# A transformer block on one core: the 128-column score row as one full-precision product, placed last, with a reordered ScalarE and VectorE

## The chip, the cores and the metric

One NeuronCore of one Trainium2 chip runs the whole kernel. The time is the device time of one execution in microseconds. Engine names: PE is TensorE, ACT is ScalarE, DVE is VectorE, POOL is GpSimd.

## What is computed

The reference, cut to what matters here (B = 16 batches of S = 512 tokens, width 128, 16 heads of 64, 8 experts with hidden size 512):

```
h = layernorm(x) * (1 + ca) + sa
q, k, v = h @ W_Q, h @ W_K, h @ W_V                  # 16 heads of 64 columns
scores  = q @ k.T / 8, causal mask, softmax over keys  # 512 x 512 for each head
x = x + ga * ((probs @ v) @ W_out + b_out)
h = layernorm(x) * (1 + cb) + sb
w = softmax over the 2 largest of h @ Wr + br
x = x + gb * sum_e w_e * (gelu(h @ W1_e + b1_e) @ W2_e + b2_e)
```

Everything is float32 in and out.

## The kernel before

**Stages.** The attention of all 16 batches comes first, then the experts of all 16 batches. In attention a batch is worked through in 8 pairs of heads, numbered 0 to 7 here; so there are 128 pairs, each the same pipeline. The change lies in this stage alone.

**Products in parts.** Most products are made of three reduced-precision products of a high and a low part: hi*hi, hi*lo, lo*hi. For q and k, ACT rounds the product in PSUM to the high part (`round_q`, `round_k`), and DVE subtracts it to get the low part (`rest_q`, `rest_k`, semaphores `q_lo` and `k_lo`). The buffers `q_hi2`, `q_lo2`, `k_hi2`, `k_lo2` hold two pairs.

**Rows and units.** The causal scores of a head are four query blocks of 128 rows. Row r needs (r + 1) * 128 key columns. They are made in three units (`UNITS`): row 3 (512 columns); rows 2 and 0 (384 and 128); row 1 (256). Each unit has its own two PSUM banks, one for each head of the pair. The two heads lie in different halves of the partitions, so their products use different halves of the array's rows (line 578).

**What PE does in a pair p**, in this order: scores of pair p in three units; `weigh_values` of pair p-2 (line 605, probabilities times V, full precision); `project_q` and `project_k` of pair p+1 (lines 523 to 525); up to two chunks of V (the same lines), none in pairs 2 and 6, two in pairs 0 and 3, one in the others; in pair 2 and pair 6 the output projection (lines 627 to 629); then 40 transposes of the probabilities of pair p-1 (line 592), in groups 2, 0, 1. The group 2 waits for all eight normalised rows of pair p-1 (`p_norm`).

**What the others do around it.** DVE (`front`, `rear`) inverts the softmax sums of pair p-1 (line 1246), adds the mask and takes the row maximum of all eight rows of pair p (line 1237), makes the low parts of z, q and k, and copies two of the three groups of transposes out of PSUM (line 1230). ACT takes the exponentials with their sums (line 954), rounds z, q and k (lines 966, 935, 939), copies the V chunks out of PSUM (line 979), and copies the third group of transposes (line 945). POOL waits for the inverted sums (`rden`) and multiplies the eight rows by them (line 501, `p_norm`). PE reads `v_done` of the last V chunk of a pair before the scores of the next, since that chunk and the score row 3 use one bank. A unit of scores waits by `t_dve` until DVE has copied the transposes that lay in its banks: unit 1 for the first copy, unit 2 for the second.

Each engine follows its own written order, and semaphores alone join them; there is no planner.

Of the kernel before, what the change touches and what calls it, by code (L numbers as in the profile page):

```python
# [17 lines left out]


ROW_ORDER = [3, 2, 0, 1]  # L20
UNITS = [[3], [2, 0], [1]]
ROW_AT = {3: 0, 2: 512, 0: 896, 1: 1024}
ROW_IN_BANK = {3: 0, 2: 0, 0: 384, 1: 0}
HEAD_COLS = 1280


# [17 lines left out]

def masked_at(h, u):

    return (h, 2 + 2 * h, 6 + h)[u]


AHEAD = [[], [2, 3], [2, 3], [2, 3], [2, 3], [2], [], [2]]  # L50
# [7 lines left out]
def adaln_moe_kernel(nc, resid, W_Q, W_K, W_V, W_out, b_out, W1, b1, W2, b2, Wr, br, c_in, wmod, out):  # L58
# [10 lines left out]
    with ExitStack() as ctx:  # L69
# [3 lines left out]
        def sem(name):  # L73
            return ctx.enter_context(nc.semaphore(name))
# [98 lines left out]
        with ExitStack() as pa:  # L173
            def sa(name, shape, dt=F32):
                return sb(name, shape, dt, pa)
# [23 lines left out]
        with ExitStack() as pb:  # L199
# [29 lines left out]
            neg_max = sa("neg_max", [P, 2, 8])  # L229
            denom = sa("denom", [P, 2, 8])  # L230
            rdenom = sa("rdenom", [P, 2, 8])

            raw_w = [v_sb[:, i, :] for i in range(3)]
            raw_wo = hidden[:, 1, 2:4, :].rearrange("p c s -> p (c s)")
# [119 lines left out]
            z_rounded = sem("z_rounded")  # L354

            q_lo = sem("q_lo")
            k_lo = sem("k_lo")
            t_dve = sem("t_dve")
            s_masked = sem("s_masked")
# [13 lines left out]
            with nc.Block() as block:  # L373
# [66 lines left out]
                @block.gpsimd  # L440
                def _(pool):
                    def inv_std(b):

                        wait_alone(pool, ln_mv, NT * b + NT)
                        pool.tensor_scalar(var_eps[:, :], meanvar[:, :, 1], EPS, 1.0, ALU.add, ALU.mult)\
                            .then_inc(ln_eps, 1)
                        pool.wait_ge(ln_eps, b + 1)
                        pool.tensor_tensor(rstd[:, :], var_eps[:, :], neg_half[:, :], ALU.pow).then_inc(ln_rstd, 1)

                    pool.memset(ident[:, :], 0.0).then_inc(pool_zero, 1)  # L450
                    pool.memset(mask_w[:, :], 0.0).then_inc(pool_zero, 1)
                    pool.memset(neg_half[:, :], -0.5).then_inc(pool_const, 1)
                    pool.wait_ge(pool_zero, 2)
                    pool.affine_select(out=ident[:, :], in_=ident[:, :], compare_op=ALU.not_equal, fill=1.0,
                                       base=0, pattern=[[-1, P]], channel_multiplier=1).then_inc(pool_const, 1)

                    pool.affine_select(out=mask_w[:, 384:512], in_=mask_w[:, 384:512], compare_op=ALU.is_ge,
                                       fill=NEG, base=0, pattern=[[-1, P]], channel_multiplier=1)\
                        .then_inc(pool_const, 1)
                    pool.wait_ge(pool_const, 1)  # L460
                    inv_std(0)
                    wo_v = W_out.rearrange("c (n two) d -> two c n d", two=2)
                    for half in range(2):
                        pool.dma_start(raw_wo[half * DH:(half + 1) * DH, :].rearrange("p (n d) -> p n d", n=NP),
                                       wo_v[half]).then_inc(load_w[3], 16)
                    pool.dma_start(bo_col[:, :], b_out.rearrange("(d o) -> d o", o=1)).then_inc(load_kept, 16)
                    pool.dma_start(br_b[:, :], br.partition_broadcast(P)).then_inc(load_kept, 16)
                    pool.dma_start(wr_sb[:, :], Wr).then_inc(load_kept, 16)
                    pool.wait_ge(load_kept, 48)

                    def router_inv_std(b):

                        wait_alone(pool, r_mv, NT * b + NT)
                        pool.tensor_scalar(var_eps[:, :], meanvar[:, :, 1], EPS, 1.0, ALU.add, ALU.mult).then_inc(r_eps, 1)
                        pool.wait_ge(r_eps, b + 1)
                        pool.tensor_tensor(rstd[:, :], var_eps[:, :], neg_half[:, :], ALU.pow).then_inc(r_rstd, 1)

                    def summed(b, e):

                        return (E - 1) * b + e  # L480

                    def add_expert(b, e):
                        wait_alone(pool, y_weighted, expert(b, e) + 1)
                        if e > 1:

                            wait_alone(pool, y_summed, summed(b, e - 1))
                        pool.tensor_tensor(acc[:, :], acc[:, :], y_w[:, :], ALU.add).then_inc(y_summed, 1)  # L487

                    def body(b, first, last):
                        for p in range(NP):  # L490
                            if p == 2 and not last:
                                inv_std(b + 1)
                            if p == 2 and last:
                                router_inv_std(0)

                            wait_alone(pool, rden, pair(1, b, p) + 1)
                            for h in range(2):
                                for r in ROW_ORDER:
                                    at, n = ROW_AT[r], (r + 1) * P
                                    part = probs[:, p % 2, h, at:at + n]  # L500
                                    pool.tensor_scalar(part, part, rdenom[:, p % 2, 4 * h + r:4 * h + r + 1], 1.0,  # L501
                                                       ALU.mult, ALU.mult)\
                                        .then_inc(p_norm, 1)

                    batches(pool, body)

                    def experts(b, first, last):
                        if not first:
                            add_expert(b - 1, E - 1)
                        if not last:  # L510
                            router_inv_std(b + 1)
                        if first:
                            pool.wait_ge(oT_ps, B)
                        for e in range(1, E - 2 if last else E - 1):
                            add_expert(b, e)

                    batches(pool, experts)

                @block.tensor
                def _(pe):  # L520
# [38 lines left out]
                    def scores(b, p, u, begin, young):  # L559
# [3 lines left out]
                            pe.wait_ge(k_lo, pair(1, b, p) + 1)  # L563
                        if young and not begin:

                            pe.wait_ge(s_masked, (2, 6, 8)[u])
                        if not young and u > 0:

                            pe.wait_ge(t_dve, pair(2, b, p) - (3, 2)[u - 1])
                        for r in UNITS[u]:  # L570
                            n = (r + 1) * P
                            at = ROW_IN_BANK[r]
                            rows = slice(r * P, (r + 1) * P)
# [35 lines left out]
                    def values(b, p, n, i):  # L609

                        t, half = i % 4, (i // 4) % 2
                        if i == 8:
                            pe.wait_ge(h_rest, b + 2)

                        pe.wait_ge(s_masked, pair(8, b, p) + (7, 2)[n])
                        toks, cols = slice(t * P, (t + 1) * P), slice(half * 512, half * 512 + 512)
                        split_product(V_BANK[n], (h_hi[:, toks], h_lo[:, toks]),
                                      (wv[0][:, cols], wv[1][:, cols])).then_inc(v_ps, 1)
# [97 lines left out]
                    def body(b, first, last):  # L716
                        for p in range(NP):
# [52 lines left out]
                                router_logits(0, k_bank)  # L770
                                project_out(b, 0, done + 2, range(2))
                            if not begin:
                                pe.wait_ge(s_masked, done + 6)
                                if p == 4 and last:
                                    attention_T_beside(b - 1)
                                if p == 5 and last:
# [143 lines left out]
                def _(act):  # L920
# [155 lines left out]
                    def front(b, p, first, last):  # L1076
# [7 lines left out]
                            round_q(*nxt, False)  # L1084
                            round_k(*nxt)
                        exponentials(b, p, 0, 1)
                        exponentials(b, p, 1, 1, [2])
                        if not (first and p < 2):
                            round_z(*two_before(b, p))
                        if has_next and not begin:  # L1090
# [7 lines left out]
                            round_w(1, 0)  # L1098
                            round_w(1, 1)
                        put = chunk_banks(p, first, last)  # L1100
                        if now:
                            values_out(b, put[0], now[0])
                        exponentials(b, p, 1, 1, [0])
                        exponentials(b, p, 0, 2)

                    def rear(b, p, first, last):
# [1 line left out]
                        prev = before(b, p)  # L1108
                        now = chunks(p, first, last)
                        put = chunk_banks(p, first, last)  # L1110
                        for n, i in zip(put[1:], now[1:]):
                            values_out(b, n, i)
                        exponentials(b, p, 1, 2)
                        if p == 5 and last:
                            act.wait_ge(t_dve, pair(2, *prev) + 1)
                            router_h_evac(0, in_halves(hf[:, :]), side)
# [3 lines left out]
                            router_round_h(0)  # L1120
                        if not begin:
                            evac_T(*prev, first and p == 1)
                        if begin:
                            round_weights(3)

# [64 lines left out]
                def _(dve):  # L1190
# [249 lines left out]

                    def front(b, p, first, last):
                        begin, nxt = first and p == 0, after(b, p)
                        if not begin:
                            invert_sums(*before(b, p))
                        mask_and_max(b, p, 0, 0)
                        mask_and_max(b, p, 1, 0)
                        mask_and_max(b, p, 0, 1)
                        if begin:
                            rest_q(*nxt)
# [141 lines left out]
```

## Time and profile before

| what | value |
|---|---|
| median of 3 runs | 1885.24 us (1884.66 to 1886.86) |
| the profiled execution's own time | 1885.15 us |
| its span | 1883.4 us, granted TensorE clock 0.997 |
| PE busy | 1869.1 us, 99% of the span |
| DVE, ACT, POOL busy | 1649.5, 1559.0, 731.9 us |
| attention stage, first scores to last transposes | 14.88 to 1148.6 us |

Busy time of PE is a union of instructions that overlap: a matmul of 512 columns is shown as 0.39 us long, while the next one starts 0.23 us after it. So a late start of up to about 0.16 us leaves no gap in PE's busy time. Distances between starts are read here instead.

### The profile page before, as it was taken

How to read it: one execution, taken by the hardware profiler on the slowest of the kernel's cores; microseconds unless marked ns; L12 is line 12 of the kernel's file. 1: busy time of each engine (PE TensorE's matmuls, PEld its weight loads, DVE VectorE, ACT ScalarE, POOL GpSimd, SP SyncE). 2: the span in 40 equal slices, each digit the busy share in tenths (PEclk: the TensorE clock that was granted, in tenths of full speed). 3: DMA queues.
4: the chain of work that ended last, by engine and by line, in shares of the span. 5: the costliest groups of instructions: out<-in, count | busy, mean ns of one | idle time of the engine just before them, and what ended most of it. 6: DMA issues, size and time to landing. Idle time of an engine off the chain costs nothing.

```text
span 1883.4 us, 50582 instructions
## 1 busy us (share of the span) xinstructions
PE 1869.1 (99%) x15334; PEld 1431.1 (76%) x15334; DVE 1649.5 (88%) x4388; ACT 1559.0 (83%) x3664; POOL 731.9 (39%) x1212
## 2 busy tenths in 40 slices
PE   8999999999999999999999999999999999999999
PEld 6777777777777777777777777888888888888887
DVE  7888888888888888888888888998998899899998
ACT  7888988988988988988988988777777777777775
POOL 4454454454444444544544442222222222222221
PEclk9999999999999999999999999999999999999999
DMA  4100000000000000000000003111111111111111
GB/s 129 62 2 1 1 1 0 1 1 0 1 1 0 1 1 0 1 1 0 1 1 1 1 2 91 52 51 50 50 50 50 50 50 50 50 50 50 51 55 52
DMA packets 42622, 50.04 MB, mean 27 GB/s; under 512 B 3160, under 2 KB 24464, under 8 KB 42512
## 3 DMA queue, kind: packets, MB, share of 16 engines
q1 hardware_dynamic: 42256, 48.41, 8.1%
q0 software_dynamic: 256, 0.53, 0.1%
q14 instruction: 86, 0.70, 0.1%
q8 instruction: 24, 0.39, 0.1%
HBM read 44.47 MB, written 4.46 MB: 26 GB/s over the span
## 4 chain that ended last, share of the span: by engine, by line
PE 97%; DVE 1%; issue 1%; ACT 1%; POOL 0%; DMA 0%; ACTq 0%; SPq 0%; DVEq 0%
PE banks L605 16%; PE banks L578 13%; PE banks L592 9%; PE banks L684 6%; PE banks L686 6%; PE banks L685 6%; PE banks L703 6%; PE banks L705 6%; PE banks L704 6%; PE banks L523 6%; PE banks L525 5%; PE banks L524 5%; PE banks L627 2%; PE banks L628 2%; PE banks L629 2%
## 5 line engine op out<-in xcount | busy, mean ns | idle before, releaser
L501 POOL TENSOR_SCALAR probs<-probs,rdenom 128x512 f32<-128x512 f32 (+3 forms) x1024 | 525.9, 540 | 586.3 <-DVE rdenom L1246 586.3
L954 ACT ACTIVATE probs<-probs,neg_max 128x512 f32<-128x512 f32 (+3 forms) x1024 | 561.6, 551 | 56.4 <-DVE neg_max L1237 56.4
L1059 ACT ACTIVATE hidden<-banks,b_cols 128x512 f32<-128x512 f32 x512 | 350.3, 689 | 177.2 <-PE banks L686 176.9
L1237 DVE CUSTOM_DVE_ANT_0 probs<-banks,mask_w 128x512 f32<-128x512 f32 (+3 forms) x1024 | 427.1, 482 | 3.9 <-PE banks L578 0.6
L1416 DVE TENSOR_TENSOR hid_lo<-hidden,hid_hi 128x512 fp32r<-128x512 f32 x512 | 380.5, 754 | 56.7 <-ACT hid_hi L1067 41.9
L487 POOL TENSOR_TENSOR acc<-acc,y_w 128x512 f32<-128x512 f32 x110 | 151.5, 1378 | 462.6 <-DVE y_w L1429 460.9
L605 PE MATMUL banks<-probs_T,v_sb 128*64 128x512 f32 (+3 forms) x2048 | 305.6, 441 | 0.3 <-issue 0.3
L1230 DVE COPY probs_T<-banks 128x512 f32<-128x512 f32 (+1 forms) x256 | 232.6, 949 | 29.7 <-PE banks L592 29.7
L605 PEld LDWEIGHTS banks<-probs_T,v_sb 128*64 128x64 f32 x2048 | 136.7, 137 | 156.3 <-issue 120.0
L592 PEld LDWEIGHTS banks<-ident,probs 64*128 64x128 f32 x5120 | 171.7, 140 | 45.5 <-issue 45.4
L684 PE MATMUL banks<-h_hi,w_hi 128*128 128x512 f32 x512 | 205.7, 402 | 0.1
L685 PE MATMUL banks<-h_hi,w_lo 128*128 128x512 f32 x512 | 199.6, 390 | 0.0
L686 PE MATMUL banks<-h_lo,w_hi 128*128 128x512 f32 x512 | 199.6, 390 | 0.0
L703 PE MATMUL banks<-hid_hi,w_hi 128*128 128x512 f32 x508 | 197.8, 389 | 0.0
L705 PE MATMUL banks<-hid_lo,w_hi 128*128 128x512 f32 x508 | 197.7, 389 | 0.0
L704 PE MATMUL banks<-hid_hi,w_lo 128*128 128x512 f32 x508 | 197.6, 389 | 0.0
L954 ACT ACTIVATION_READ_ACCUMULATOR probs<-probs,neg_max 128x1 f32 x1024 | 192.5, 188 | 0.0
L592 PE MATMUL banks<-ident,probs 64*128 64x64 f32 x5120 | 189.2, 226 | 0.8 <-ACT hidden L1059 0.6
L578 PE MATMUL banks<-k_hi,q_hi 64*128 64x512 f32 (+3 forms) x1024 | 177.3, 342 | 4.2 <-DVE probs_T L1230 2.1
L1250 DVE TENSOR_TENSOR z_lo<-banks,z_hi 128x512 fp32r<-128x512 f32 x128 | 88.3, 690 | 90.3 <-ACT z_hi L966 88.4
L578 PE MATMUL banks<-k_hi,q_lo 64*128 64x512 f32 (+3 forms) x1024 | 166.0, 319 | 0.0
L945 ACT ACTIVATE probs_T<-banks 128x1024 f32<-128x1024 f32 x128 | 129.8, 1014 | 43.5 <-PE banks L592 43.5
(182 smaller groups left out, 3425.9 us busy)
## 6 DMA issues: line engine op xcount, KB each, us to landing
w_rows<-w_kept SPq DMA_DIRECT2D x128, 256.0 KB, 4.3
x_all<-in_L_attn_resid_dram SPq DMA_DIRECT2D x16, 256.0 KB, 2.7
w_raw<-in_L_ffn_W_dram SPq DMA_DIRECT2D x16, 256.0 KB, 4.7
out_dram<-y_result SPq DMA_DIRECT2D x15, 256.0 KB, 2.3
v_sb<-in_L_attn_W_V_dram SPq DMA_DIRECT2D x1, 512.0 KB, 5.7
hidden<-in_L_attn_W_out_dram POOLq DMA_DIRECT2D x2, 256.0 KB, 6.4
v_sb<-in_L_attn_W_Q_dram SPq DMA_DIRECT2D x1, 448.0 KB, 3.4
v_sb<-in_L_attn_W_K_dram SPq DMA_DIRECT2D x1, 448.0 KB, 4.4
```

The costliest lines, as they stand in the source:

```text
L501: pool.tensor_scalar(part, part, rdenom[:, p % 2, 4 * h + r:4 * h + r + 1], 1.0, ALU.mult, ALU.mult)\
L578: mm = pe.matmul(S_BANK[u][h][:, at:at + n], q[own, p % 2, rows], k[own, p % 2, 0:n], start=start, stop=stop)
L592: mm = pe.transpose(banks[:, first_bank + half, at:at + DH], probs[own, p % 2, h, src:src + P], ident[own, own])
L605: mm = pe.matmul(bank[h * DH:(h + 1) * DH, c * P:S], v_sb[:, c, hc:hc + DH], probs_T[:, h, KEY_AT[c]:KEY_AT[c] + n], start=(c == 0), stop= ...
L684: pe.matmul(banks[:, c, :], w1_hi[:, e, cols], h_hi[:, :], start=True, stop=False)
L685: pe.matmul(banks[:, c, :], w1_lo[:, e, cols], h_hi[:, :], start=False, stop=False)
L686: pe.matmul(banks[:, c, :], w1_hi[:, e, cols], h_lo[:, :], start=False, stop=True)\
L703: pe.matmul(y_bank, w2_hi[:, e, c, :], hi, start=(c == 0), stop=False)
L954: act.activation(part, part, ACT.Exp, bias=neg_max[:, p % 2, col:col + 1], scale=-1.0, accum_out=denom[:, p % 2, col:col + 1]).then_inc(p_ ...
L1059: act.activation(hidden[:, e % 2, c, :], banks[:, c, :], ACT.Gelu, bias=b1_cols[:, e * HC + c:e * HC + c + 1]).then_inc(hid, 1)
L1237: dve.tensor_tensor_reduce(out=probs[:, p % 2, h, at:at + n], in0=S_BANK[u][h][:, col:col + n], in1=mask_w[:, 512 - n:512], scale=-SCALE, ...
L1416: dve.tensor_tensor(hid_lo[:, e % 2, c, :], full, hi.bitcast(F32), ALU.subtract)\
```

## The change

Score row 0 moves out of the middle unit to the end of the last one, behind row 1, and becomes one full-precision float32 product of `q_full` and `k_full` per head instead of three products of parts. POOL makes `q_full` and `k_full` (128 columns each) as the sum of the high and the low part, behind its eight multiplications of a pair, and tells by `q_whole` and `k_whole`. ACT copies both V chunks of a pair ahead of the last exponentials, and copies its group of transposes ahead of the last head's exponentials (two of them now). DVE inverts the sums of the pair before behind the first two masks instead of ahead of them. Semaphore counts follow.

```diff
-UNITS = [[3], [2, 0], [1]]
+UNITS = [[3], [2], [1, 0]]
-ROW_IN_BANK = {3: 0, 2: 0, 0: 384, 1: 0}
+ROW_IN_BANK = {3: 0, 2: 0, 0: 256, 1: 0}
...
-    return (h, 2 + 2 * h, 6 + h)[u]
+    return (h, 2 + h, 4 + 2 * h)[u]
...
                                         .then_inc(p_norm, 1)
+                            if not (last and p >= NP - 2):
+                                join(*after(*after(b, p)))
+
+                    def join(b, p):
+
+                        wait_alone(pool, q_lo, pair(1, b, p) + 1)
+                        pool.tensor_tensor(q_full[:, p % 2, :], q_hi2[:, p % 2, 0:P].bitcast(F32),
+                                           q_lo2[:, p % 2, 0:P].bitcast(F32), ALU.add).then_inc(q_whole, 1)
+                        wait_alone(pool, k_lo, pair(1, b, p) + 1)
+                        pool.tensor_tensor(k_full[:, p % 2, :], k_hi2[:, p % 2, 0:P].bitcast(F32),
+                                           k_lo2[:, p % 2, 0:P].bitcast(F32), ALU.add).then_inc(k_whole, 1)
+
+                    join(0, 0)
+                    join(0, 1)
                     batches(pool, body)
...
-                            pe.wait_ge(s_masked, (2, 6, 8)[u])
+                            pe.wait_ge(s_masked, (2, 4, 8)[u])
...
                         for r in UNITS[u]:
+                            if r == 0:
+                                pe.wait_ge(q_whole, pair(1, b, p) + 1)
+                                pe.wait_ge(k_whole, pair(1, b, p) + 1)
+                                at = ROW_IN_BANK[0]
+                                for h in range(2):
+                                    own = slice(h * DH, (h + 1) * DH)
+                                    mm = pe.matmul(S_BANK[u][h][:, at:at + P], q_full[own, p % 2, :],
+                                                   k_full[own, p % 2, :], start=True, stop=True)
+                                continue
...
-                        pe.wait_ge(s_masked, pair(8, b, p) + (7, 2)[n])
+                        pe.wait_ge(s_masked, pair(8, b, p) + (6, 2)[n])
...
-                                pe.wait_ge(s_masked, done + 6)
+                                pe.wait_ge(s_masked, done + 4)
...
                         exponentials(b, p, 0, 1)
-                        exponentials(b, p, 1, 1, [2])
+                        exponentials(b, p, 1, 1)
...
-                        if now:
-                            values_out(b, put[0], now[0])
-                        exponentials(b, p, 1, 1, [0])
+                        for bank, i in zip(put[:2], now[:2]):
+                            values_out(b, bank, i)
                         exponentials(b, p, 0, 2)
...
-                        for n, i in zip(put[1:], now[1:]):
+                        for n, i in zip(put[2:], now[2:]):
                             values_out(b, n, i)
-                        exponentials(b, p, 1, 2)
+                        if begin:
+                            exponentials(b, p, 1, 2)
...
                         if not begin:
                             evac_T(*prev, first and p == 1)
+                            exponentials(b, p, 1, 2)
...
                         begin, nxt = first and p == 0, after(b, p)
+                        mask_and_max(b, p, 0, 0)
+                        mask_and_max(b, p, 1, 0)
                         if not begin:
                             invert_sums(*before(b, p))
-                        mask_and_max(b, p, 0, 0)
-                        mask_and_max(b, p, 1, 0)
                         mask_and_max(b, p, 0, 1)
```

## Rows read from the trace of the kernel before

**Rows 1.** The profile's page: span, chain that ended last, two groups of POOL.

```profile
span 1883.4 us, 50582 instructions
PE 97%; DVE 1%; issue 1%; ACT 1%; POOL 0%; DMA 0%; ACTq 0%; SPq 0%; DVEq 0%
L487 POOL TENSOR_TENSOR acc<-acc,y_w 128x512 f32<-128x512 f32 x110 | 151.5, 1378 | 462.6 <-DVE y_w L1429 460.9
```

**Rows 2.** Waits of PE: who waited for whom; us in total, times, longest.

```profile
PE banks L592 <- POOL probs L501: 0.2, 1, 0.2
```

**Rows 3.** Timeline of PE, scores of one pair 3; start us, length us, what.

```profile
602.79 0.48 PE L578 MATMUL banks<-k_hi,q_hi 64*128 64x512 f32 x2
...
603.92 0.33 PE L578 MATMUL banks<-k_lo,q_hi 64*128 64x384 f32 x2
604.10 0.22 PE L578 MATMUL banks<-k_hi,q_hi 64*128 64x128 f32 x2
...
604.38 0.34 PE L578 MATMUL banks<-k_hi,q_hi 64*128 64x256 f32 x2
604.55 0.28 PE L578 MATMUL banks<-k_hi,q_lo 64*128 64x256 f32 x2
604.67 0.28 PE L578 MATMUL banks<-k_lo,q_hi 64*128 64x256 f32 x2
604.88 2.38 PE L605 MATMUL banks<-probs_T,v_sb 128*64 128x512 f32 x16
```

**Rows 4.** Timeline of PE: a run of full-precision products of 128 columns.

```profile
12.90 2.05 PE L798 MATMUL banks<-mask_w,ident 128*128 128x128 f32 x16
```

**Rows 5.** Timeline of DVE, pairs 3 to 5.

```profile
602.40 1.81 DVE L1230 COPY probs_T<-banks 128x512 f32<-128x512 f32 x2
...
612.37 0.19 DVE L1246 RECIPROCAL rdenom<-denom 128x8 f32<-128x8 f32 x1
612.67 0.69 DVE L1237 CUSTOM_DVE_ANT_0 probs<-banks,mask_w 128x512 f32<-128x512 f32 x1
...
613.90 0.55 DVE L1237 CUSTOM_DVE_ANT_0 probs<-banks,mask_w 128x384 f32<-128x384 f32 x1
...
618.30 0.69 DVE L1223 TENSOR_TENSOR k_lo<-banks,k_hi 128x512 fp32r<-128x512 f32 x1
```

**Rows 6.** Timeline of POOL: eight multiplications each, in pairs 4 and 5.

```profile
612.73 4.10 POOL L501 TENSOR_SCALAR probs<-probs,rdenom 128x512 f32<-128x512 f32 x8 [4.14 <-DVE rdenom L1246]
621.00 4.10 POOL L501 TENSOR_SCALAR probs<-probs,rdenom 128x512 f32<-128x512 f32 x8 [4.18 <-DVE rdenom L1246]
```

**Rows 7.** Timeline of PE: transposes and the scores behind them, pairs 3 to 5.

```profile
610.13 1.49 PE L592 MATMUL banks<-ident,probs 64*128 64x64 f32 x40
611.56 0.50 PE L578 MATMUL banks<-k_hi,q_hi 64*128 64x512 f32 x2
...
618.25 1.48 PE L592 MATMUL banks<-ident,probs 64*128 64x64 f32 x40
619.53 0.48 PE L578 MATMUL banks<-k_hi,q_hi 64*128 64x512 f32 x2
...
626.20 1.47 PE L592 MATMUL banks<-ident,probs 64*128 64x64 f32 x40
```

**Rows 8.** Timeline of ACT, end of pair 3 and end of pair 6.

```profile
610.93 0.58 ACT L979 ACTIVATE v_sb<-banks 128x512 f32<-128x512 f32 x1
611.40 0.50 ACT L954 ACTIVATE probs<-probs,neg_max 128x256 f32<-128x256 f32 x1
...
638.58 1.03 ACT L945 ACTIVATE probs_T<-banks 128x1024 f32<-128x1024 f32 x1 [0.51 <-PE banks L592]
```

**Rows 9.** Timelines at the end of attention: ACT, POOL, PE.

```profile
1140.02 1.02 ACT L945 ACTIVATE probs_T<-banks 128x1024 f32<-128x1024 f32 x1 [0.87 <-PE banks L592]
...
1141.11 5.07 POOL L501 TENSOR_SCALAR probs<-probs,rdenom 128x512 f32<-128x512 f32 x8 [5.32 <-DVE rdenom L1246]
...
1146.33 0.47 PE L592 MATMUL banks<-ident,probs 64*128 64x64 f32 x8 [0.20 <-POOL probs L501]
```

More of the change, by code:

```diff
@@ L231, in adaln_moe_kernel @@
             rdenom = sa("rdenom", [P, 2, 8])
+            q_full = sa("q_full", [P, 2, P])
+            k_full = sa("k_full", [P, 2, P])
             raw_w = [v_sb[:, i, :] for i in range(3)]
@@ L356, in adaln_moe_kernel @@
             q_lo = sem("q_lo")
+            q_whole, k_whole = sem("q_whole"), sem("k_whole")
             k_lo = sem("k_lo")
```

## The prediction, made before the changed kernel ran

> **What bounds the kernel now.** First the page: the chain that ended last is PE for 97% of the span [rows 1]. Then the waits of PE: POOL made it wait once, for 0.2 us, in the whole run [rows 2]. Both say that PE alone sets the time, and both hide how near the others are. So I read, third, the timelines of each engine over one batch and lay them side by side, all measured from the first score matmul of a pair (call it S). The first scores stand at 14.88 us and the experts begin at about 1149, so a pair takes some 8.8 us on average, and by the timeline a pair with one V chunk (pairs 1, 4, 5, 7) takes 7.97: pair 4 runs from 611.56 to 619.53 [rows 7].
>
> In pair 4 the transposes start at 618.25, S + 6.69 [rows 7]. They need all eight rows of the pair before from POOL. POOL works from 612.73 for 4.10 us, to 616.83 [rows 6]: 1.42 us early. In pair 5 they start at 626.20, S + 6.67, and POOL ends at 625.10: 1.10 us early. This slack is the number on which everything below turns. POOL starts 0.17 us behind the end of the reciprocal (612.37 + 0.19 = 612.56, then 612.73) [rows 5, 6].
>
> **Row 0 on PE.** Before, in its place: row 2's last product starts at 603.92, row 0's first at 604.10 and row 1's first at 604.38, so row 0 costs 0.28 us for three products of both heads, side by side [rows 3]. Row 1's three start at 604.38, 604.55, 604.67: 0.17 and 0.12 apart, where the first is longer since its weights were only being loaded behind row 0's short products. From row 2's last start to row 1's last start it is 0.75 us. After: row 1's weights load beneath row 2's 384 columns, so 0.17 to its first product and 0.12 twice; then row 0. A full-precision product shows as two instructions. A run of 16 of 128 columns lasts 2.05 us; with 0.38 off for the last one's length and the first weight load, 15 steps in 1.67, 0.11 each [rows 4]. The products of probabilities and V are full precision too, two heads in different columns of the array: 16 instructions in 2.38 us [rows 3] is 8 steps, the heads side by side. If the heads are side by side here as well, row 0 is 0.12 + 0.11, and the sum from row 2's last start to the last start of the unit is 0.17 + 0.24 + 0.12 + 0.11 = 0.64, 0.11 less than 0.75. The trace has no full-precision product of two heads in different rows of the array. The bounds: side by side, -0.11 us for a pair; one head behind the other, four steps instead of two, +0.11. I take the first, since line 578's own products and line 605's both run in step.
>
> The row speaks of weight loads (0.11 a step) as the limit at 128 columns. The Trainium skill, FP8 and Floating Point Precision, section TensorE Precision Notes, says that true FP32 takes four passes through the array (H*H + H*L + L*H + L*L). By that count the product would grow from three passes to four of 128 columns, and would lose where I have it gain; a step of 0.11 for two passes of 128 columns fits its count, but the three reduced products took 0.28, not the 0.16 of three passes, so here the count does not set the price.
>
> The two new waits ahead of row 0: what is queued behind is row 0, then `weigh_values`. `k_lo` of pair 5 ends at 618.30 + 0.69 = 618.99 [rows 5]; POOL wakes 0.17 later and adds. Its addition of 128 columns is bounded from above by one of 512 columns, 1.38 us [rows 1], from below by nothing. So `k_whole` comes at 619.2 to 620.5, and row 0 is due at S + 1.5 = 621.0 [rows 7]. No cost at either end. POOL's additions stand behind its multiplications, and POOL then idles 4.1 us [rows 6]: no cost either.
>
> **The second V chunk.** In pair 3 ACT ends it at 610.93 + 0.58 = 611.51, and the scores start at 611.56 [rows 7, 8]: 0.05 us is the way from ACT to PE. Transposes to scores is 1.43 us there (610.13 to 611.56) against 1.28 in pair 4 (618.25 to 619.53), and the late scores pay 0.02 more for weights not loaded ahead. One exponential of about 0.4 us stands ahead of the chunk that then stands behind. So 0.17 us goes in pairs 0 and 3 each. Next in line there is PE itself.
>
> **Transposed copy ahead of exponentials, on ACT.** Where ACT is free it starts this copy at S + 0.23 (638.58 in pair 7, with its scores at 638.35) and takes 1.03 [rows 8]. The two exponentials moved behind it (0.49 and 0.39 to their next) end at about S + 2.15, plus 0.05 on the way. Now the sums of the pair before are complete only there, instead of before S.
>
> **The reciprocal moved on DVE.** This is the step that costs. Before, it ran ahead of the masks: 612.37 in pair 4, S + 0.81, and at S + 1.11 in pair 5 (POOL's 621.00 less 0.17 and 0.19 [rows 6]). After, it stands behind two masks of 512 columns, which start at S + 1.09 to 1.11, when unit 0 is done (612.67 in pair 4), and take to 613.90, 1.23 us [rows 5]. So: 1.09 + 1.23 = S + 2.32 (the exponentials' S + 2.20 is hidden by it), + 0.19 for itself, + 0.17 until POOL starts = 2.68, + 4.10 = 6.78, + 0.15 from POOL's end to the transposes (1141.11 + 5.07 = 1146.18, then 1146.33 [rows 9]) = S + 6.93. PE would be there at 6.67 - 0.11 = 6.56. So pairs 1, 4, 5, 7 start their transposes at 6.93, not at 6.67 or 6.69: 0.25 us later than before, whatever PE gains in row 0. What is queued behind the wait is all that remains of the pair and the next pair's scores: a closed loop of scores, masks, reciprocal, POOL, transposes, 6.93 + 1.28 = 8.21 us instead of 7.96. In pairs 0, 2, 3, 6 PE has a second V chunk or a projection to do first, arrives at 7.2 or later (pair 3: 610.13 - 602.79 = 7.34, less 0.11) and is not held.
>
> **The unit moved forward.** Row 1 now starts behind row 2 and needs the second DVE copy out of its banks. In pair 3 it ends at 602.40 + 1.81 = 604.21, + 0.05 = S + 1.47 [rows 5]; with 0.11 for the weights the first product of row 1 can start at S + 1.58, and before it started at 1.59 (604.38), just free. Now it is due at 603.92 + 0.17, S + 1.30 [rows 3]: 0.28 us lost. This is in pair 3 only. Elsewhere the copy ends 2.3 us behind the transposes' start (610.13, and 612.37 + 0.08 for the reciprocal behind it [rows 5, 7]), which is S + 1.04 of the next pair, where the transposes themselves are what DVE waits for.
>
> **The sum for a batch**: pairs 1, 4, 5, 7: 4 * 0.25 = +1.0. Pairs 2 and 6: -0.22. Pair 0: -0.11 - 0.17 = -0.28. Pair 3: -0.11 - 0.17 + 0.28 = 0. Together +0.5; times 16, +8.0. The first batch has DVE further behind and its loop is later for it: +1, my estimate. At the end of attention ACT waits 0.87 us for its transposes (to 1140.02) with the exponentials done [rows 9]; now two of them come behind, so the sums, POOL and ACT's next work are some 0.9 later, and PE waits there already: +0.9. Sum +9.9, on the profiled execution's own 1885.15 (span 1883.4, 1.75 around it), which lies 0.1 below the median: 1895.1 us.
>
> **Rivals.** (1) *The heads of row 0 run one behind the other.* For: nothing in the trace shows them side by side in this form. Against: rows 3. It costs 0.22 more where PE is the bound, pairs 0, 2, 3, 6: 64 * 0.22 = 14; in the others 6.78 stays below 6.93. 1909. Four passes by count, 0.05 more instead of 0.11 less, would give 64 * 0.16 = 10 more, 1905. (2) *The loop through POOL doesn't bind, and the change brings what PE gains.* It needs POOL's end at S + 6.4 instead of 6.78, as when the reciprocal starts by S + 1.95: between the masks, or with masks a third shorter. Against: three durations that hardly vary (masks, 4.10, 0.15). From 0.38 us less it decides, and the time is the other side's: -0.11 in eight pairs, -0.17 in two, +0.28 in pair 3, and some 0.08 back in four for the copy that unit 2 now waits for: -0.6 a batch, -10, 1875. (3) *The loop binds, but less*, as latencies overlap: half the 0.25 gives 64 * 0.12 = 8 less, 1887, hardly told from no change.
>
> **How the numbers follow.** Forecast, with its own range 1890 to 1900: 0.62. Rival 1 with its form by passes: 0.16. Rival 2: 0.10. Rival 3: 0.12. A measurement of this kernel tells 0.2%, 3.8 us. Faster by more: rival 2, 0.10. Within: most of rival 3, 0.10. Slower: 0.80. The range, 1887 to 1906, leaves out rival 2 and the serial end of rival 1.
>
> **What would show it.** Right: waits of PE on POOL's line 501, about 64 of them, in pairs 1, 4, 5, 7; transposes at S + 6.9 there; reciprocal at S + 2.3; POOL's end 0.15 ahead of the transposes. Line 578's last unit 0.64 long from row 2's last start; row 0's two heads within 0.01 us. Pair 3 to 4: transposes to scores 1.28, and a DVE wait at unit 2 in pair 3. Wrong: no wait on POOL, or masks that start ahead of S + 1.0.

## The result, and the profile after

| | before | changed |
|---|---|---|
| median (19 runs each) | 1885.11 us (1882.86 to 1887.39) | 1889.87 us (1887.97 to 1891.26) |
| ratio to the kernel before, 95% interval | | 1.0025 (1.0018 to 1.0031) |
| span of the profiled execution | 1883.4 us | 1889.4 us |

Slower by 4.8 us, where 1895.1, slower by 9.9, was forecast. The direction and the mechanism came out, the size did not.

The page of the changed kernel (span; busy times; the chain; one group of POOL):

```profile
span 1889.4 us, 50738 instructions
...
PE 1856.6 (98%) x15078; PEld 1424.6 (75%) x15078; DVE 1669.1 (88%) x4388; ACT 1563.9 (83%) x3664; POOL 850.2 (45%) x1468
...
PE 96%; issue 2%; DVE 1%; ACT 1%; POOL 0%; DMA 0%; ACTq 0%; DVEq 0%; POOLq 0%
```

PE is busy for 12.5 us less and the kernel takes longer: the gain on PE is there, and "issue" has grown from 1% to 2% [rows 1]. The waits of PE in the changed kernel (us in total, times, longest) say where:

```profile
PE banks L617 <- issue: 19.0, 64, 1.1
...
PE banks L603 <- DVE probs_T L1256: 1.6, 5, 0.3
PE banks L617 <- POOL probs L504: 1.4, 1, 1.4
```

Line 617 are the transposes (592 before). They waited 64 times: 56 times in pairs 1, 4, 5, 7 of the 14 middle batches, about 0.27 us each, and eight times in the first and the last batch, the longest 1.06 us; before, once [rows 2]. The view puts this down to "issue": a bare wait instruction stands between POOL's signal and the transposes, and only the timelines of both engines show who ended it. First PE, pair 3 to pair 5, which answers to [rows 3, 7]:

```profile
607.84 0.34 PE L603 MATMUL banks<-k_lo,q_hi 64*128 64x384 f32 x2
608.18 0.39 PE L603 MATMUL banks<-k_hi,q_hi 64*128 64x256 f32 x2
...
614.20 1.47 PE L617 MATMUL banks<-ident,probs 64*128 64x64 f32 x40
615.48 0.48 PE L603 MATMUL banks<-k_hi,q_hi 64*128 64x512 f32 x2
...
616.62 0.33 PE L603 MATMUL banks<-k_lo,q_hi 64*128 64x384 f32 x2
616.79 0.28 PE L603 MATMUL banks<-k_hi,q_hi 64*128 64x256 f32 x2
616.91 0.28 PE L603 MATMUL banks<-k_hi,q_lo 64*128 64x256 f32 x2
617.02 0.28 PE L603 MATMUL banks<-k_lo,q_hi 64*128 64x256 f32 x2
617.14 0.38 PE L593 MATMUL banks<-k_full,q_full 64*128 64x128 f32 x4
617.46 2.37 PE L630 MATMUL banks<-probs_T,v_sb 128*64 128x512 f32 x16
...
622.38 1.43 PE L617 MATMUL banks<-ident,probs 64*128 64x64 f32 x39 [0.28 <-issue]
623.61 0.47 PE L603 MATMUL banks<-k_hi,q_hi 64*128 64x512 f32 x1
...
630.54 1.48 PE L617 MATMUL banks<-ident,probs 64*128 64x64 f32 x40 [0.27 <-issue]
```

Then DVE and POOL in the same stretch, which answers to [rows 5, 6]:

```profile
606.31 1.81 DVE L1256 COPY probs_T<-banks 128x512 f32<-128x512 f32 x2
...
616.58 0.69 DVE L1263 CUSTOM_DVE_ANT_0 probs<-banks,mask_w 128x512 f32<-128x512 f32 x1
...
617.81 0.20 DVE L1272 RECIPROCAL rdenom<-denom 128x8 f32<-128x8 f32 x1
```

```profile
618.18 4.10 POOL L504 TENSOR_SCALAR probs<-probs,rdenom 128x512 f32<-128x512 f32 x8 [3.31 <-DVE rdenom L1272]
622.33 0.46 POOL L513 TENSOR_TENSOR q_full<-q_hi,q_lo 128x128 f32<-128x128 f32 x1
622.92 0.46 POOL L516 TENSOR_TENSOR k_full<-k_hi,k_lo 128x128 f32<-128x128 f32 x1
626.34 4.10 POOL L504 TENSOR_SCALAR probs<-probs,rdenom 128x512 f32<-128x512 f32 x8 [2.96 <-DVE rdenom L1272]
```

In pair 4 the scores start at 615.48 (S), the masks at S + 1.10, the reciprocal at S + 2.33, POOL runs from S + 2.70 to 622.28 = S + 6.80, and the transposes start at S + 6.90: 0.10 behind POOL. This is the closed loop. Row 0 at 617.14 has both heads side by side: four instructions in 0.38 us.

The distance from scores to scores, pair by pair, read from the starts on PE's timeline (medians of batches 2 to 14; us):

```
pair          0     1     2     3     4     5     6     7
before      8.78  7.97  9.99  8.78  7.97  7.95 10.87  7.95
forecast    8.50  8.22  9.88  8.78  8.22  8.20 10.76  8.20
changed     8.54  8.16  9.91  8.78  8.13  8.18 10.79  8.14
```

A batch takes 70.64 us instead of 70.27, +0.37, where +0.5 was forecast. Of the 5 us by which the forecast was too high, 1.8 lie in these middle batches and the rest in the first batch and at the end of attention, worked out below.

### The profile page after: what moved, and what is told of

It reads as the page before. It is cut to its first block, busy times and chain, and to the rows that moved or that the text cites. A ratio compares the mean times of both kernels' runs of the same rounds, so it can differ in the third digit from the quotient of the medians.

```text
span 1889.4 us, 50738 instructions
## 1 busy us (share of the span) xinstructions
PE 1856.6 (98%) x15078; PEld 1424.6 (75%) x15078; DVE 1669.1 (88%) x4388; ACT 1563.9 (83%) x3664; POOL 850.2 (45%) x1468
## 4 chain that ended last, share of the span: by engine, by line
PE 96%; issue 2%; DVE 1%; ACT 1%; POOL 0%; DMA 0%; ACTq 0%; DVEq 0%; POOLq 0%
PE banks L630 15%; PE banks L603 11%; PE banks L617 9%; PE banks L709 6%; PE banks L710 6%; PE banks L711 6%; PE banks L728 6%; PE banks L730 6%; PE banks L729 6%; PE banks L539 6%; PE banks L540 5%; PE banks L541 4%; PE banks L652 2%; PE banks L653 2%; PE banks L654 2%
## 5 line engine op out<-in xcount | busy, mean ns | idle before, releaser
L1263 DVE CUSTOM_DVE_ANT_0 probs<-banks,mask_w 128x512 f32<-128x512 f32 (+3 forms) x1024 | 434.6, 480 | 6.9 <-PE banks L603 0.7
L1092 ACT ACTIVATE hid_hi<-hidden 128x512 fp32r<-128x512 f32 x256 | 161.0, 629 | 0.0
L603 PE MATMUL banks<-k_hi,q_hi 64*128 64x512 f32 (+2 forms) x768 | 150.4, 367 | 3.5 <-DVE q_lo L1243 1.6
```

The lines of the kernel that those rows point to most:

```text
L603: mm = pe.matmul(S_BANK[u][h][:, at:at + n], q[own, p % 2, rows], k[own, p % 2, 0:n], start=start, stop=stop)
L1263: dve.tensor_tensor_reduce(out=probs[:, p % 2, h, at:at + n], in0=S_BANK[u][h][:, col:col + n], in1=mask_w[:, 512 - n:512], scale=-SCALE, ...
```

## The experiments

The parts of the change were run alone and undone one by one, then the loop itself was lengthened, shortened and opened. Each ran in turn with the kernel before (1884 to 1885 us); ratios have 95% intervals. The changed kernel did not run again in these rounds: differences to it are taken from its median above, 1889.87, and since the kernel before was up to 1.25 us faster here than there, they are certain to about 1 us only. The theory under test: the added time comes only from the loop of scores, masks, reciprocal, POOL and transposes in the pairs 1, 4, 5, 7.

**The sooner V chunk alone.**

```diff
-                        if now:
-                            values_out(b, put[0], now[0])
+                        for bank, i in zip(put[:2], now[:2]):
+                            values_out(b, bank, i)
...
-                        for n, i in zip(put[1:], now[1:]):
+                        for n, i in zip(put[2:], now[2:]):
```

> The kernel before with one part alone: ACT copies both V chunks ahead of the last exponentials. The loop theory (the added time comes only from the loop scores, masks, reciprocal, POOL, transposes) has this part as a pure gain: transposes to scores 1.28 us instead of 1.43 in pairs 0 and 3, 0.17 us each with the weights, 32 times, -5.4 us. Rival, that ACT's order is where the changed kernel loses: then this is no gain or a loss, 0 or above.

1878.28 us, ratio 0.9964 (0.9950 to 0.9977), -6.7. Pairs 0 and 3 fall from 8.78 to 8.64, pairs 1 and 4 from 7.97 to 7.95. This part is a gain and by itself the faster kernel.

**The late reciprocal alone.**

```diff
-                        if not begin:
-                            invert_sums(*before(b, p))
                         mask_and_max(b, p, 0, 0)
                         mask_and_max(b, p, 1, 0)
+                        if not begin:
+                            invert_sums(*before(b, p))
```

> The kernel before with one part alone: the sums are inverted behind the first two masks. Loop theory: in pairs 1, 4, 5, 7 the transposes start at 6.9 us behind the scores' start instead of 6.67, about 0.2 us more each, 64 times, +13 us, and a few more in the first batch. Rival, that the loss comes from row 0's product or from ACT: then there is no change here, within 2 us.

1896.63 us, ratio 1.0060 (1.0047 to 1.0074), +11.6. Its timelines of POOL and PE at a pair 5:

```profile
629.91 4.10 POOL L501 TENSOR_SCALAR probs<-probs,rdenom 128x512 f32<-128x512 f32 x8 [4.07 <-DVE rdenom L1246]
```

```profile
634.11 1.47 PE L592 MATMUL banks<-ident,probs 64*128 64x64 f32 x40 [0.16 <-issue]
635.36 0.50 PE L578 MATMUL banks<-k_hi,q_hi 64*128 64x512 f32 x2
```

POOL ends at 634.01, the transposes start 0.10 later, 6.9 behind their scores. One reciprocal, moved behind two masks on DVE, costs more than the whole change does.

**Both of these.**

```diff
-                        if now:
-                            values_out(b, put[0], now[0])
+                        for bank, i in zip(put[:2], now[:2]):
+                            values_out(b, bank, i)
...
+                        mask_and_max(b, p, 0, 0)
+                        mask_and_max(b, p, 1, 0)
                         if not begin:
                             invert_sums(*before(b, p))
-                        mask_and_max(b, p, 0, 0)
-                        mask_and_max(b, p, 1, 0)
```

> The kernel before with two parts: the reciprocal behind the first two masks and the sooner V chunk. If the parts add up: +11.6 (the reciprocal alone) - 6.7 (V alone) = +4.9, 1889 to 1890, the changed kernel's own time, which means that row 0's place, its product and ACT's other order come to nothing together. If the late reciprocal takes away what the V chunk gives (the same pairs held by POOL): 1893 or more.

1891.01 us, ratio 1.0035 (1.0022 to 1.0049), +7.2 where the sum of the two is +4.9, which the interval just holds. So the two add up nearly or wholly, and what remains of the change (row 0's place, its product, ACT's other order) is worth about -1 us in all (1889.87 less 1891.01), or -2.4 if each kernel is held against the kernel before of its own round.

**Row 0 in parts, everything else as changed.**

```diff
-                            if r == 0:
-                                pe.wait_ge(q_whole, pair(1, b, p) + 1)
-                                pe.wait_ge(k_whole, pair(1, b, p) + 1)
...
-                                join(*after(*after(b, p)))
...
```

> The changed kernel, but row 0 stays three products of parts in its new place (last), and POOL makes no sums. Loop theory: pairs 1, 4, 5, 7 don't notice, since POOL holds them; pairs 0, 2, 3, 6 lose the 0.08 to 0.11 us that the one product gains: 64 * 0.1, +5 to +6 us against the changed kernel, 1895. Rival, that POOL's sums or the two added waits delay something: at or below the changed kernel.

1894.08 us, ratio 1.0050 (1.0037 to 1.0064): 4.2 above the changed kernel, where 5 to 6 was expected. Pairs 1, 4, 5, 7 are unchanged at 8.15 to 8.17, pairs 0, 2, 3, 6 are 8.61, 9.98, 8.87, 10.86, 0.07 to 0.09 more each. The one product gains where PE is the bound and nothing where POOL is. The rest of the remainder, place and ACT's order, costs about 3.

**Row 0 and the V chunk, with ACT and DVE in their old order.**

```diff
-                        if begin:
-                            exponentials(b, p, 1, 2)
+                        exponentials(b, p, 1, 2)
...
-                            exponentials(b, p, 1, 2)
...
+                        if not begin:
+                            invert_sums(*before(b, p))
                         mask_and_max(b, p, 0, 0)
...
```

> The changed kernel with two parts undone: the reciprocal ahead of the masks again, and ACT's last two exponentials ahead of its transposed copy again. Row 0's product and the sooner V chunk stay. Loop theory: POOL ends at 5.6 us behind the scores' start and holds nobody; the scores gain 0.08 in all eight pairs, 0.15 in pairs 0 and 3, and give 0.28 back in pair 3 where unit 2 waits for a DVE copy: -0.6 us a batch, about -10 against the kernel before, unless ACT's copy now comes too late for the weighted values. Rival, that row 0's product costs more than it saves: above the kernel before.

1889.68 us, ratio 1.0026 (1.0015 to 1.0036): a miss; I had named the doubt and put the time on the other side of it. With row 0 in the last unit, the last head has two exponentials ahead of ACT's transposed copy. PE in a pair 4 (its scores start at 615.10), then ACT:

```profile
615.10 0.47 PE L603 MATMUL banks<-k_hi,q_hi 64*128 64x512 f32 x1
...
617.27 2.38 PE L630 MATMUL banks<-probs_T,v_sb 128*64 128x512 f32 x16
```

```profile
616.17 1.00 ACT L970 ACTIVATE probs_T<-banks 128x1024 f32<-128x1024 f32 x1
```

The copy ends at 617.17, S + 2.07, and the weighted values start 0.10 later, at S + 2.17 instead of 1.98. The sums are complete late too, so the masks start at S + 1.41 instead of 1.10. The loop through POOL is open here (its end is at S + 5.73 in this pair and near 5.65 in most), and the time is the changed kernel's all the same.

**Row 0's part alone on the kernel before.**

```diff
-UNITS = [[3], [2, 0], [1]]
+UNITS = [[3], [2], [1, 0]]
...
+                                    mm = pe.matmul(S_BANK[u][h][:, at:at + P], q_full[own, p % 2, :],
...
```

> The kernel before with row 0's part alone (its place, the one product, POOL's sums), ACT and DVE in their old order. By the run that also had the sooner V chunk (1889.7): ACT has two exponentials of the last head ahead of its transposed copy, ends this at 2.08 us behind the scores' start, and the weighted values wait for it. Without the sooner V chunk pairs 0 and 3 pay more, since one exponential more stands ahead of it: 0.3 us or more each, +10 us against that run, 1899. Rival, that the product by itself is a gain: below 1885.

1890.61 us, ratio 1.0036 (1.0022 to 1.0050), 0.9 above the run before it and not 10. Pairs 0 and 3 pay 0.15 each for the late V chunk, half of what was expected; in return pairs 1 and 4 behind them take 7.85 and 7.87 instead of 8.03, since ACT has done one exponential more by then and its copy starts at S + 0.72 instead of 1.08. I had counted the first, at twice its size, and not the second. The rival falls too: row 0's part as a whole (place, product, sums) is no gain while ACT and DVE keep their old order. Of the product alone this run says nothing; the run with row 0 in parts does.

**The reciprocal put back, ACT as changed.**

```diff
+                        if not begin:
+                            invert_sums(*before(b, p))
                         mask_and_max(b, p, 0, 0)
                         mask_and_max(b, p, 1, 0)
-                        if not begin:
-                            invert_sums(*before(b, p))
```

> The changed kernel with the reciprocal alone put back ahead of the masks; ACT still takes the last head's two exponentials behind its transposed copy, so the sums are complete only at about 2.2 us behind the scores' start. DVE stands at the reciprocal until then: reciprocal from 2.2, POOL from 2.55 to 6.65, 0.15 earlier than in the changed kernel, but the masks begin at 2.4 instead of 1.1, and the exponentials, the rounding of z and what follows them on ACT come 1 us later. Loop theory with this: slower than the changed kernel, 1900 or more, so the move of the reciprocal is the price of ACT's order. Rival, that the place of the reciprocal alone is at fault: faster than the changed kernel.

1926.29 us, ratio 1.0223 (1.0209 to 1.0237). DVE's timeline in a pair 2:

```profile
614.96 0.20 DVE L1272 RECIPROCAL rdenom<-denom 128x8 f32<-128x8 f32 x1 [0.48 <-ACT probs L979]
615.16 0.69 DVE L1263 CUSTOM_DVE_ANT_0 probs<-banks,mask_w 128x512 f32<-128x512 f32 x1
```

DVE stands still for ACT's sums with eight masks queued behind. With ACT's order as changed, the reciprocal can't stay in front: the one move enforces the other. The loop through POOL does not explain this time, for POOL's end lies at S + 6.72 in a pair 4, ahead of the 6.80 of the changed kernel. There DVE, then PE:

```profile
634.47 0.20 DVE L1272 RECIPROCAL rdenom<-denom 128x8 f32<-128x8 f32 x1 [1.21 <-ACT probs L979]
...
639.84 0.68 DVE L1249 TENSOR_TENSOR k_lo<-banks,k_hi 128x512 fp32r<-128x512 f32 x1
```

```profile
640.67 0.50 PE L603 MATMUL banks<-k_hi,q_hi 64*128 64x512 f32 x2
```

DVE waits 1.21 us, then works without a gap from the reciprocal to the low part of k, which ends at 640.52, and the next scores, which need it, start 0.15 later. This is a second closed loop (scores, ACT's sums, reciprocal, masks, DVE's low parts), and it takes 8.39 us. Pairs 0, 2, 3 and 6 are 0.3 to 0.4 longer too; what holds them was not followed.

**One of POOL's eight multiplications left out.** Row 2 of the second head stays unnormalised.

```diff
                                 for r in ROW_ORDER:
+                                    if (h, r) == (1, 2):
+                                        continue
...
-                                wait_alone(pe, p_norm, pair(8, *prev) + 8)
+                                wait_alone(pe, p_norm, pair(7, *prev) + 7)
```

> The changed kernel, but POOL leaves out one of its eight multiplications (row 2 of the second head is not normalised), which takes 0.56 us off its 4.10. Loop theory: POOL ends at 6.25 instead of 6.8, PE reaches the transposes at 6.59 by itself, and pairs 1, 4, 5, 7 fall to 7.87 us: 0.3 us each, 64 times, -19 us against the changed kernel, so -14 against the kernel before. Rival, that POOL's work is off the path: no change against the changed kernel, +5 against the kernel before.

1871.73 us, ratio 0.9928 (0.9915 to 0.9942): -18.1 against the changed kernel, -19 expected. Its POOL and PE in a pair 4:

```profile
607.33 3.54 POOL L506 TENSOR_SCALAR probs<-probs,rdenom 128x512 f32<-128x512 f32 x7 [3.31 <-DVE rdenom L1274]
```

```profile
604.63 0.48 PE L605 MATMUL banks<-k_hi,q_hi 64*128 64x512 f32 x2
611.18 1.47 PE L619 MATMUL banks<-ident,probs 64*128 64x64 f32 x40
612.46 0.48 PE L605 MATMUL banks<-k_hi,q_hi 64*128 64x512 f32 x2
```

POOL ends at 610.87, PE reaches its transposes at S + 6.55 by itself: 7.83 us for the pair.

**One multiplication more.**

```diff
+            spare_cols = sa("spare_cols", [P, P])
...
                             wait_alone(pool, rden, pair(1, b, p) + 1)
+                            pool.tensor_scalar(spare_cols[:, :], ident[:, :], 1.0, 1.0, ALU.mult, ALU.mult)
```

> The changed kernel with one more multiplication of 128 columns on POOL, to a tile that nobody reads, ahead of its eight (some 0.36 us). Loop theory: pairs 1, 4, 5, 7 pay it in full, 64 * 0.36 = +23 us against the changed kernel, pairs 0 and 3 next to nothing, pairs 2 and 6 nothing: 1913. Rival, that POOL only happens to end there: no change, 1890.

1906.33 us, ratio 1.0116 (1.0100 to 1.0131): 16.5 above the changed kernel instead of 23. The added instruction and the next, on POOL:

```profile
634.71 0.30 POOL L501 TENSOR_SCALAR spare_cols<-ident 128x128 f32<-128x128 f32 x1 [2.96 <-DVE rdenom L1274]
634.98 4.08 POOL L506 TENSOR_SCALAR probs<-probs,rdenom 128x512 f32<-128x512 f32 x8
```

It takes 0.27 us and not 0.36. POOL's end moves by 0.25, from S + 6.79 to 7.04, pairs 1, 4, 5, 7 by 0.24 to 0.25 (8.38 to 8.42), the other four by 0.02 or less: 64 * 0.25 = 16. Only the instruction was priced too high.

**The sums inverted head by head.**

```diff
+                    def invert_head(b, p, h):
+                        dve.wait_ge(p_exp, pair(8, b, p) + 6 + 2 * h)
+                        dve.reciprocal(rdenom[:, p % 2, 4 * h:4 * h + 4], denom[:, p % 2, 4 * h:4 * h + 4])\
+                            .then_inc(rden, 1)
...
+                        if not begin:
+                            invert_head(*before(b, p), 0)
                         mask_and_max(b, p, 0, 0)
                         mask_and_max(b, p, 1, 0)
                         if not begin:
-                            invert_sums(*before(b, p))
+                            invert_head(*before(b, p), 1)
...
-                            wait_alone(pool, rden, pair(1, b, p) + 1)
                             for h in range(2):
+                                wait_alone(pool, rden, pair(2, b, p) + h + 1)
```

> The changed kernel, with the sums inverted for each head: head 0 ahead of the masks (its exponentials are done there), head 1 behind the first two masks; POOL begins with head 0's four rows at once. Everything else as changed. Loop theory: POOL starts at about 1.4 us behind the scores' start, goes on with head 1 without a stop and ends at 5.5 instead of 6.8, pairs 1, 4, 5, 7 fall from 8.15 to about 7.87 us, and the time comes near that with seven multiplications: 1872, 13 below the kernel before. Rival, that DVE is as near to the path as POOL: the second reciprocal costs 0.1 to 0.2 us in each pair and the time stays above 1878.

1872.42 us, ratio 0.9939 (0.9925 to 0.9953): 11.6 below the kernel before, 17.5 below the changed one. The first head's sums are complete ahead of ACT's copy, so POOL begins with them and finds the second head's ready. POOL and PE, a pair 4:

```profile
607.35 4.10 POOL L504 TENSOR_SCALAR probs<-probs,rdenom 128x512 f32<-128x512 f32 x8 [1.91 <-DVE rdenom L1276]
```

```profile
612.59 1.47 PE L617 MATMUL banks<-ident,probs 64*128 64x64 f32 x40
613.88 0.48 PE L603 MATMUL banks<-k_hi,q_hi 64*128 64x512 f32 x2
```

Eight multiplications without a stop, done 1.14 us ahead of the transposes; pair 4 takes 7.83, a batch 69.46. It keeps every part of the change and beats both kernels.

## Why the prediction was right in kind and wrong in size

**The loop** (the reciprocal moved on DVE): shown. Started later alone it costs +11.6; lengthened by 0.27 on POOL it costs 16.5 more, shortened it gives 18.1, opened 17.5. Its places were forecast as S + 2.32 for the reciprocal, 2.68 to 6.78 for POOL; measured 2.33, 2.70, 6.80. What failed are three terms of the sum, all too high: "pairs 1, 4, 5, 7: 4 * 0.25 = +1.0", the +1 for the first batch, and the +0.9 for the end of attention; the last two are taken up below. The first of the three measured 0.19, 0.16, 0.23, 0.19 (the table), +0.77: over 14 batches 3.2 us less than forecast, of which 1.4 is hidden because pairs 0, 2 and 6 gained 0.10 less than forecast. Two parts of it were mis-sized. From POOL's end to the transposes it is 0.10 and not 0.15; the 0.15 came from one row [rows 9]. And from the transposes to the next scores it is 1.23 to 1.25 and not 1.28 where PE has waited (622.38 to 623.61). This is so in the run with the late reciprocal too (634.11 to 635.36, 1.25), and not in the one where the loop is open (612.59 to 613.88, 1.29). I had carried 1.28 over from transposes that never waited. Why they run closer behind a wait was not tried.

**Row 0 on PE**: right in form, side by side (rival 1 falls). From row 2's last start (616.62) to the last products it is as worked out, 0.17, 0.12, 0.11, 0.12. What pairs 2 and 6 gained was 0.08 and not 0.11 each. Nearly all of it is the product: with row 0 moved but still in parts pair 2 takes 9.98, 0.01 less than before. The count of passes in rival 1, by which the product would lose, had it the wrong way round: the one product is worth -4.2 us. POOL's sums took 0.46 us each and held nobody.

**The second V chunk**: forecast 0.17 in pairs 0 and 3, -5.4; alone it measured 0.14 there and 0.02 in the pairs behind them, -4.2 over the 14 middle batches. Its median fell by 6.7. Of the rest its trace shows 2.2 us behind the last batch's first scores, and 1.7 of these lie in products that the account of the ends below tells of.

**The unit moved forward**: shown in the trace only. In pair 3 the copy ends at 606.31 + 1.81 = 608.12, and row 1 starts at 608.18 with its weights not loaded, against 0.17 behind row 2 in pair 4. Pair 3 stayed at 8.78, as forecast.

**The ends of attention**, which I set at +1 for the first batch and +0.9 for the end: the first batch is 0.56 longer in all (forecast 1.5), and the stretch from the last batch's scores to the end is 0.9 shorter (forecast +1.4). I had not looked at the last pair. There POOL holds PE as worked out, and more: for 1.38 us instead of 0.20 [rows 9] at the last transposes, and for 0.95 at those ahead of them. Against this stand two gains. First, the weighted values of the last pair start at S + 3.0 instead of 4.1, since DVE's copies there end at S + 2.2 instead of 3.5; DVE waits for ACT's rounding of the router's input, which stands behind the moved exponentials. Two of the runs differ in ACT's order alone and bear this out: the weighted values start at S + 5.28 with ACT's old order (row 0 and the V chunk) and at S + 3.57 with the new one (the reciprocal put back):

```profile
1139.03 2.93 PE L630 MATMUL banks<-probs_T,v_sb 128*64 128x512 f32 x16
```

```profile
1171.92 2.37 PE L630 MATMUL banks<-probs_T,v_sb 128*64 128x512 f32 x16
```

Second, these same sixteen products took 4.07 us in the trace before and 2.37 in the one after:

```profile
1132.02 4.07 PE L605 MATMUL banks<-probs_T,v_sb 128*64 128x512 f32 x16
```

```profile
1138.10 2.37 PE L630 MATMUL banks<-probs_T,v_sb 128*64 128x512 f32 x16
```

They take 2.37 to 2.38 with the V chunk alone and with the late reciprocal alone as well. So 1.7 us of the end is nothing that the change was meant to do, and without it the end would be 0.8 longer; why the trace before has it is open.

**The books.** Between the two traces: 14 middle batches +5.2 (forecast 7.0), first batch +0.6 (1.5), last one to the end -0.9 (1.4), and +1.1 ahead of the first scores (0): 6.0, the difference of the spans. The 1.1 is of the execution: eight products on PE that wait for nothing took 2.06 us there and 1.37 before, and in the twelve traces of this case the first scores stand anywhere from 13.56 to 16.21 us. Without it 4.9 is left, and the medians differ by 4.8. That this agrees so well is in part luck, for the 1.7 us at the end may be of the execution too.

By the parts: reciprocal +11.6, V chunk -6.7, row 0's one product -4.2, which makes +0.7. The changed kernel stands at +4.8, so +4.1 is left for row 0's place, ACT's order and whatever doesn't add up. The run with two parts puts the place and the order at about 3 and the other 1 to 2 at the way in which reciprocal and V chunk add. No run has ACT's order alone on the kernel before.

## What to carry to other kernels

An engine that never makes the bound wait may be one short delay from it: measure, from the start of a repeated stage, when each helper ends and when the bound engine needs it, and hold every moved instruction against that slack. A helper's job that waits for a whole set of inputs can often be cut so that it begins with the part that is ready; here one reciprocal made two gave back 17.5 us. When a loop through a helper becomes the bound, what the bound engine saves inside it is worth nothing, so price such savings only in the stages outside it.

## What was not expected of the hardware

Forty transposes take 1.28 us to the next scores when PE runs into them and 1.23 to 1.25 when it had waited for them. In the waits view a wait behind a bare wait instruction is told as "issue" (19.0 us, 64 times), where both timelines show POOL 0.10 us ahead. The stretch ahead of the first scores varies by execution: 14.88 us in the trace before, 15.98 in the one after, where the same eight products of 128 columns took 1.37 and 2.06 us, and twelve traces range from 13.56 to 16.21 us:

```profile
9.03 2.06 PE L823 MATMUL banks<-mask_w,ident 128*128 128x128 f32 x8
```
